# The degree column in 32 pieces of four table rows, two a turn, with twelve groups' places scattered in the node run

## The reference, cut to what matters

```python
deg = segment_sum(edge_weight, src, n)
dinv = where(deg > 0, 1 / sqrt(where(deg > 0, deg, 1)), 0)
w = -(dinv[src] * edge_weight * dinv[dst])
prop = lambda h: segment_sum(w[:, None] * h[src], dst, n)
```

## Time and profile before

| | us |
|---|---|
| median of 3 runs (5558.6 to 5562.95) | 5559.81 |
| the profiled execution | 5550.47 |
| its span, first to last instruction | 5548.7 |
| DVE busy | 4082.3 (74%) |
| POOL busy | 3649.7 (66%) |
| PE busy | 3567.5 (64%) |
| ACT busy | 2607.1 (47%) |

### The profile page before, as it was taken

How to read it: one execution, slowest core, us unless ns; L and a number is a source line. 1 busy time by engine, 2 the same in 40 slices (tenths; PEclk the granted TensorE clock), 3 DMA queues, 4 the chain that set the end, 5 groups by cost and what they waited for, 6 DMA issues and landing times. The chain is left out here.

```text
span 5548.7 us, 71528 instructions
## 1 busy us (share of the span) xinstructions
PE 3567.5 (64%) x15267; PEld 1836.1 (33%) x15267; DVE 4082.3 (74%) x6661; ACT 2607.1 (47%) x5644; POOL 3649.7 (66%) x3646
## 2 busy tenths in 40 slices
PE   8992788847776999677628867777555545651110
PEld 5551555523332333244314433333222212221000
DVE  8873788847774555699879969999655569996442
ACT  6662677733331222476629963344222247772221
POOL 7776277757775777577723447666377767765777
PEclk9996899978885555699959989999655668885555
DMA  7539977744442222466514433232244423322221
GB/s 103 70 62 43 117 235 230 229 140 105 108 106 52 62 62 62 137 208 199 184 56 141 136 94 80 83 83 83 85 133 133 125 67 78 77 69 65 71 73 49
DMA packets 535687, 595.54 MB, mean 107 GB/s; under 512 B 297570, under 2 KB 312040, under 8 KB 533947
## 3 DMA queue, kind: packets, MB, share of 16 engines
q1 hardware_dynamic: 319036, 473.91, 28.9%
q0 software_dynamic: 112896, 91.81, 8.4%
q10 hardware_dynamic: 103648, 28.71, 6.3%
HBM read 354.69 MB, written 303.31 MB: 119 GB/s over the span
## 5 line engine op out<-in xcount | busy, mean ns | idle before, releaser
L1152 POOL DMA_INDIRECT l_got<-d_x,l_near x1176 | 1159.0, 986 | 555.3 <-issue 357.1
L1160 POOL DMA_INDIRECT ln_xd<-d_xt,idsE x392 | 369.9, 944 | 204.3 <-issue 119.2
L1152 POOL DMA_INDIRECT p_got<-d_sums,p_near x392 | 401.8, 1025 | 151.8 <-issue 147.8
L2473 POOL DMA_INDIRECT out<-fi_res,fi_near x392 | 381.0, 972 | 182.1 <-issue 118.8
L935 POOL DMA_INDIRECT d_pos<-placeE,finE x392 | 401.0, 1023 | 147.5 <-issue 136.8
L1152 POOL DMA_INDIRECT p_got<-d_ext,p_near x392 | 380.9, 972 | 163.6 <-issue 117.7
L1152 POOL DMA_INDIRECT p_got<-d_h,p_near x392 | 383.7, 979 | 155.8 <-issue 116.4
L883 PE MATMUL ps<-hot_lo,hot_w 128*128 128x392 bf16 x2352 | 393.0, 331 | 16.0 <-ACT hot_w L917 16.0
L2147 PE MATMUL ps<-l_hid,w2n 128*64 128x512 f32 x392 | 236.1, 760 | 162.5 <-DVE l_sums L1325 156.0
L917 ACT ACTIVATE hot_w<-hot_hi,vals 128x128 bf16<-128x128 bf16 x784 | 268.8, 393 | 125.6 <-DVE hot_lo L784 114.8
L411 PE MATMUL ps<-ident,fi_sums 64*128 64x64 f32 x392 | 53.2, 315 | 425.2 <-DVE fi_sums L1325 425.2
(11 more groups left out here) (392 smaller groups left out, 10786.3 us busy)
## 6 DMA issues: line engine op xcount, KB each, us to landing
l_xd<-d_x SPq DMA_DIRECT2D x147, 256.0 KB, 2.9
d_ext<-ln_ext SPq DMA_DIRECT2D x98, 264.0 KB, 2.2
d_xt<-in_x_wide ACTq DMA_DIRECT2D x49, 520.0 KB
ln_x<-in_x SPq DMA_DIRECT2D x98, 256.0 KB
d_h<-ln_hb SPq DMA_DIRECT2D x98, 256.0 KB, 2.7
d_x<-ln_x SPq DMA_DIRECT2D x98, 256.0 KB
lb_x<-d_x SPq DMA_DIRECT2D x49, 512.0 KB
d_x<-lb_x SPq DMA_DIRECT2D x49, 512.0 KB
```

Source lines behind the costliest of these rows:

```text
L1152: nc.gpsimd.indirect_dma_start(out=out[:, q], out_offset=None, in_=source, in_offset=bass.IndirectOffsetOnAxis(ap=ids[:, q:q + 1], axis=0) ...
L1160: nc.gpsimd.indirect_dma_start(out=out[:, q], out_offset=None, in_=source, in_offset=bass.IndirectOffsetOnAxis(ap=ids[:, g, q:q + 1], axis ...
L2473: nc.gpsimd.indirect_dma_start(out=out, out_offset=bass.IndirectOffsetOnAxis(ap=near[:, r, q:q + 1], axis=0), in_=res[:, r, q], in_offset= ...
```

## The change

The column is cut by table rows and not by table columns: 32 pieces of four rows, each 4 x 784 numbers, and ScalarE issues two pieces at the head of each of its first 16 turns. The degree stage scatters the places of 37 groups, the node run those of twelve. Tails (and with them the stores of `ext`) come two steps later, the stores of gathered rows four.

```diff
-PLACED_EARLY = 40
+PLACED_EARLY = 37
 PLACED_LATE = GROUPS - PLACED_EARLY
-COLUMN_PARTS = 16
+COLUMN_PARTS = 32
+COLUMNS_A_TURN = 2
-TAIL_LATE = 18
+TAIL_LATE = 20
 EXT_LATE = TAIL_LATE + 5
 def xd_turn(e):
-    return 22 + 17 * (e + 1) // 10
+    return 26 + 17 * (e + 1) // 10
...
-        column = D.xt.rearrange("(h k l) c -> k h l c", k=COLUMN_PARTS, l=TABLE_COLS // COLUMN_PARTS)[:, :, :, C:C + 1]
-        factors = W.tab[:].rearrange("h (k l) -> h k l", k=COLUMN_PARTS)
+        column = D.xt.rearrange("(h l) c -> h l c", l=TABLE_COLS)[:, :, C:C + 1]
+        part_rows = P // COLUMN_PARTS
...
                 def columns(i, r, g):
-                    if isinstance(g, int) and g < COLUMN_PARTS:
-                        act.dma_start(column[g], factors[:, g].unsqueeze(2), allow_slow_non_contiguous=True
-                                      ).then_inc(m["columns"], 16)
+                    for k in range(COLUMNS_A_TURN):
+                        if isinstance(g, int) and g * COLUMNS_A_TURN + k < COLUMN_PARTS:
+                            at = part_rows * (g * COLUMNS_A_TURN + k)
+                            act.dma_start(column[at:at + part_rows], W.tab[at:at + part_rows].unsqueeze(2),
+                                          allow_slow_non_contiguous=True).then_inc(m["columns"], 16)
```

## The result

The changed kernel takes 5740.4 us (median; 5737.0 to 5749.8) against 5559.2 us: a ratio of 1.0327, 95% interval 1.0314 to 1.0341. The direction is the predicted one; the size, +181 us, is five times the predicted +36. The profiled execution has a span of 5740.0 us, 191.3 more than before, and three places of the trace account for it.

The account below looks back on a forecast made before the run. The prediction took ScalarE's blocking column issues, 10.25 us a turn, to bound the node run's first 16 turns; -30.6 (places) + 2.9 (tails) + 64 (column) = +36 gave 5596 us, range 5530 to 5710.

Parts of the forecast that it names:

- Places, -30.6: End of degree stage: 24 scatters at 1.276 us leave it, so the node run starts 30.6 us earlier.
- SyncE's -33.5: End of degree stage: the most the moved scatters could gain if GpSimd's drain were shorter, since SyncE drains at 426.9.
- Tails, +2.9: End of node run: two more tail steps at 1.45 us add 2.9 us; later stores of gathered rows cost nothing.
- The column, four engines: Column in the node run: a four-row piece uses four engines, 25,088 elements each; four engines with gaps, +64 us, chance 0.47.
- The rival with all sixteen engines: Column: elements spread over all sixteen engines, column turns stay at 164 us; 5532 us, perhaps 5463; chance 0.20.
- The column, the time of one engine: Column: 6.0 ns an element on one engine, 6.7 us a piece with its start, last issue returning after 228 us.
- 2.0 us of start: Column: each piece's own elements start 2.0 us after the issue before it returns, a gap charged for every piece.
- the slow rival: Column: one engine's pace stays at 39 elements per us, +476 us, 6008 us in all; above 5680 us chance 0.18.
- The bounds of that term: Column: its +64 us could be +26 without gaps, or +137 with 2.5 us gaps and all SyncE packets at 160 ns.
- The third rival: Column: the pace of one engine does not rise; 640 us, +476, sum 6008 us; above 5680 us chance 0.18.
- Memory is then less loaded: Column: reason for a value near the low bound, 470 elements per us asked of memory against 629 before.
- Marks: Signs in the new trace: start near 430.6, 100,480 packets, 32 bursts after 2 us pauses, last issue after 228, GpSimd waiting 110.

Follow-up runs that it names:

- e2: The changed kernel with the old constants (40 early groups, tails and stores of gathered rows as before): ratio 1.0376 to the kernel before.
- e9: The changed kernel with each four-row piece cut into four DMAs, every fourth table column in one: 5875.3 us, ratio 1.0574 to the kernel before.
- e6: The changed kernel with 64 column pieces of two table rows, four a turn: 5977.7 us in one run, against 5557.6 for the kernel before.
- e3: The changed kernel with 16 column pieces of eight table rows, one a turn: 5597.8 us, ratio 1.0052 to the kernel before.
- e4: The changed kernel with 8 column pieces of sixteen table rows, one a turn in the first eight turns: 5575.5 us, ratio 1.0002 to the kernel before.

## Why the prediction was right and wrong

**What bounds the kernel.** Right: the column issue on ScalarE is what the first 16 turns wait for; e2 puts the whole loss there.

**Places, -30.6.** Measured -33.0. The 24 scatters were counted right; it is the drain that was taken as it stood. GpSimd's drain was 5.78 us and not 7.74, which brought the sum to within half a us of the named floor, SyncE's -33.5. Why it is shorter stays open.

**Tails, +2.9.** Measured 5.1 (e2 against the change). The price of a step was right, the last tail loads after the change are 1.44 us apart:

```profile
1350.72 0.43 SPq L996 DMA_DIRECT2D ln_tail<-d_dinv  x1
1352.16 0.43 SPq L996 DMA_DIRECT2D ln_tail<-d_dinv  x1
```

What was put at nothing is the later stores of gathered rows. Three of them (1334.68, 1338.09 and 1341.54 us) now stand among the last tails in SyncE's order, where before there was one (1146.53), at some 0.5 us each. That is 1 us of the 2.2 that are missing; the rest was not traced. Small either way.

**The column, four engines.** Right, and it holds for single elements: 100,480 packets, as forecast, and e9's 100,864. The rival with all sixteen engines falls.

**The column, the time of one engine.** This is the step that failed: "a piece then takes 784 x 6.0 = 4.7 us behind its 2.0 us of start". An element takes 14.5 ns on an engine beside the scatters, starts of pieces included: 784 x 14.5 = 11.4 us instead of 6.7. (Alone it is 13.4 ns, 10.5 us a piece, and 0.4 us to the next.) Over 31 pieces that is 146 us. The rest of the sum was near: 31 x 11.4 = 353 leaves 32 us of the 384.6 for all else, SyncE's packets above all, where 21 of at most 43 were charged. 146 + 11 = 157, which is 384.6 - 228.

The 2.0 us of start were misread as well, and this error went the other way. In the 2.0 us in which the column moved 50 packets, SyncE's took 92.0% of the time of sixteen engines: that time is SyncE's packets, which were charged a second time among the 21 us, and not a start.

Why 6.0 was the wrong row: it was read from the last 28 elements of the column, as if one engine had moved them one after the other. The row does not say that: 9.3% of sixteen engines over 0.17 us is 0.25 us of packet time, more than the stretch is long, so at times two packets were under way. A better figure was at hand: 5821 packets in 4.8 us, 76 per us and engine, 13 ns, in a stretch behind the scatters. The prediction used it as an argument against the slow rival instead of as a price: 784 / 76 = 10.3 us a piece gives 31 x 10.3 + 21 = 340 us, and 402 with the pause; the truth lies between. That 76 comes so near the 74 after the change is in part luck: it is the mean of a rate that falls within those 4.8 us.

**The bounds of that term.** Both ends (+26 and +137) kept the 6.0 ns and varied only pauses and SyncE's packets, so the range did not hold the term that was least known. Between 6.0 ns and the third rival's 25.4 there was a gap of a factor of four, and all of it above 5680 us was priced as one rival with a chance of 0.18. The result fell there.

**"Memory is then less loaded".** This reason did not hold. With the column's packets alone an engine moves 74 elements per us where four run and where eight run, and 73 at best where sixteen run: with fewer engines it does not come near the 6.0 ns, 167 per us. Four engines make 298 in all, far from the 1170 that sixteen reached, so it is not memory's total that held them. And the 629 was read as memory's pace from a stretch without SyncE's packets in which GpSimd scattered.

**The third rival.** It said that the pace of one engine does not rise. It did, from 39 to 69 per us in stretches beside the scatters, so the column's 16 turns grew by 220.6 us and not by 476. Its mark, issues of 20 us and more each, did not come: 11.2 us at the median, two a turn of 24 us.

**Marks.** Start 428.2 (430.6 named), 100,480 packets: right. A burst behind a pause of 2 us for each piece, a last issue after 228 us, a wait of 110 us on GpSimd: wrong, with 0.4 us from piece to piece, 384.6 and 276.2.

## What to carry to other kernels

Before a DMA of many small elements is cut anew, count the engines that its outermost size allows (the completion packets of a similar DMA show it), and price the elements per engine by a stretch of hundreds of them in which no other queue has packets, never by the closest few. A stretch is undisturbed only when all queues have been looked at: here the longest one without SyncE's packets held GpSimd's, and its 39 per us and engine, 25.4 ns, would have been nearly as wrong a price as the 6.0 ns. When the trace offers two paces that lie far apart, both belong into the bounds of the forecast's own sum. And a part of a change can be good while the whole is bad: here the moved scatters gain 33 us and the new cut loses 220.6, so the parts are worth running one by one.

## What the runs showed of the hardware

Elements of 4 bytes, 260 bytes apart in HBM; the engines by the completions of a piece (its rows). First in 16 us with GpSimd's scatters and without SyncE's packets (e6 from 500 to 516 us, the others as above), then in the stretches in which the column's packets are alone:

| engines | kernel | beside scatters, per us | per engine | alone, per us | per engine | ns an element on one |
|---|---|---|---|---|---|---|
| 2 | e6 | 163 | 81 | 169 | 84 | 11.8 |
| 4 | after | 276 | 69 | 298 | 74 | 13.4 |
| 8 | e3 | 472 | 59 | 595 | 74 | 13.5 |
| 16 | e4 | 643 | 40 | 794 to 1170 | 50 to 73 | 14 to 20 |
| 16, old cut | before | 629 | 39 | no long stretch | | |

Alone, two to eight engines bring elements nearly in proportion to their number. Sixteen hold that pace in one stretch of 4 us and fall to 50 in one of 10. Beside the scatters the pace of an engine is lower, and the more so the more engines a piece has (81 to 40); that the scatters are the reason was not tried apart. The number of engines is not all: e9, with 1040 bytes from one element to the next and DMAs of a quarter of the size, moves 195 per us on four engines, and some of the change's own pieces 251. What an engine waits for between two elements stays open: no view shows it.

With the paces alone all but one of a kernel's pieces would take 326 us after the change, 158 in e3 and 584 in e6; the column turns took 384.6, 235.9 and 614.8. The 30 to 78 us more in each hold the scatters, SyncE's packets and the starts of pieces, not taken apart.

A second queue on a four-row piece adds 7% beside the scatters (295 against 276) and 14% alone (340 against 298), and holds up the loads and stores of the engine that carries it. GpSimd's drain behind the scatters took 5.78 us in all nine traces with 37 groups in the degree stage, and 7.74 in the two with 40 (before, e2).
